# Transposing an even query tile one slot later, together with its odd neighbour

## The chip, the cores and the metric

One core of one Trainium2 chip runs the whole program. The metric is device time in microseconds (us) from start to end of one execution. The engines are named as the profile names them: PE is TensorE's matrix multiply, PEld its weight load, DVE is VectorE, ACT ScalarE, POOL GpSimd, SP the engine that issues the transfers (its queue is SPq).

## The reference, cut to what matters

The input is 32 images of 128 channels by 56 x 56 pixels, float32. Two residual layers follow each other. The first multiplies each channel of the group-normalised image by a gate, which comes from a small deformable convolution over the pooled channels. The second is local attention:

```python
value = conv1x1(x, v_w, v_b)
keyf = proj(x, k...); query = proj(x, q...)       # two 1x1 convs with batch norm and relu each, 64 channels
uk = concat([unfold3(keyf, d) for d in (1, 2, 4)]) # 27 neighbours of each pixel, dilations 1, 2, 4
uv = concat([unfold3(value, d) for d in (1, 2, 4)])
sim = softmax(sum(uk * query[:, :, None], axis=1, keepdims=True), axis=2)
context = sum(sim * uv, axis=2)
return conv1x1(context, w_w, w_b)                  # added to x
```

## The kernel before, in words

**Tiles.** An image is cut into 7 strips of 8 columns, a strip into 7 units of 8 x 8 pixels. Two units are the 128 queries of one tile (128 partitions); 49 units give 25 tiles, 0 to 24, the last one half full. The neighbours of a unit lie in a window of 16 x 16 pixels, so the scores of a tile are 128 queries by 256 keys.

**The path of one tile.** `scores` (L401, one matmul at L416, 256 columns) writes the scores to PSUM (`ps_s`, two banks). `masked` on DVE (L924, L929) adds a mask, takes the row's minimum of the negated scores (`zmin`) and writes `e` in SBUF, a ring of 5 buffers. `exponentials` on ACT (L580, L584) takes the exponential with its row sum. `reciprocals` and `scaled` on DVE (L934, L939; lines 937, 943 and 946) normalise it. `transposed` on PE (L420, L428) turns the 128 x 256 tile into two 128 x 128 transposes, written into a PSUM bank `ps_t` that an even tile and the odd tile after it share. `copy` on ACT (L587, L599) moves both of them, 512 columns, to `eT` in SBUF at once. `context` on PE (L433; L449 and L454) multiplies `eT` with the values into `ps_o`, and `final` on DVE (L950, L954) adds the result to the image.

**The order of the work is written out by hand.** There are 25 slots per image, one per tile, and each engine runs its own list of calls per slot. The stages lag: in slot t, `scores(t)`, `masked(t)` and `exponentials(t)` run; scaling is of tile t - 1, transposing of tile t - 3, context of tile t - 5 (`SCALE, TRANSPOSE, CONTEXT, FINAL = 1, 3, 5, 6`, L45). A lag past the start of an image goes to the last tiles of the image before. On PE the slot is, in this order (L543 to L565): `scores`, `transposed`, then if due `hidden` and `values`, `context`, if due `query_and_key`, and small matmuls of the gate's chain of steps (L505 to L523).

**What prepares the next strips.** Seven times per image PE runs `hidden` (L460, the matmul at L466, 448 columns) for a strip, ACT writes `hid` (L634), in the next slot PE runs `query_and_key` (L469, L471), and ACT writes the keys `kk` (L621) and the queries `qq` (L610), all through one PSUM bank `ps_p`. With `G_SLOT` (L47), `hidden` runs in slots 1, 4, 8, 11, 15, 19 and 22, and `query_and_key` in slots 2, 5, 9, 12, 16, 20 and 23. `values` (L474, L489) runs in slots 4, 7, 10, 17, 18, 21 and 24. One slot later than `query_and_key`, SP copies keys within SBUF: L355 (`kk<-kk`) and, for three tiles whose two units lie in different strips (tiles 3, 10 and 17), L359 and L361 (`ksp<-kk`). `scores` of such a tile waits for them (L404). SP also stores the finished image (`store`, L343, L345) in slot 5 of the next image, ahead of the key copies of slot 6.

**ACT's slot** (L623 to L638): `copy`, if the tile t - 3 is odd or is tile 24, then `exponentials(t)`, then `hid`, or `kk` and `qq`, where due, then steps of the gate's chain (L645, L650). Since tile t - 3 is odd in even slots, the copies come in the even slots 4 to 24, in slot 1 (tiles 22 and 23) and in slot 2 (tile 24 alone).

**DVE's slot** (L1031 to L1050): reciprocal of tile t - 1, `masked(t)`, `scaled` of tile t - 1, chain steps, `final`, and the write-back of the values (L967).

Of the kernel before, what the change touches and what calls it, by code (L numbers as in the profile page):

```python
# [36 lines left out]
TILES = 25  # L37
# [107 lines left out]
def lagged(n, t, lag):  # L145

    return (n, t - lag) if t >= lag else (n + -1, t - lag + TILES)
# [11 lines left out]
def build(nc, x, par, w1, w2, wv, wo, bo, bv, wg, out):  # L159
    with ExitStack() as ctx:  # L160
# [141 lines left out]
        def items_at(n, t):  # L302

            for m, rel in ((n, t), (n + 1, t - TILES)):
                if m.exists():
                    yield m, rel

        def chain_at(n, t):

            for m, rel in ((n + 1, t + TILES), (n + 2, t), (n + 3, t - TILES)):  # L310
                if m.exists():
                    yield m, rel
# [10 lines left out]
        def images(first, last, drain=0, register=None):  # L323

            with nc.Block() as block:
# [74 lines left out]
                def _(pe):  # L400
                    def scores(n, t):  # L401
                        s, u = half_tile(2 * t)
                        if special(t):
                            pe.wait_ge(k_copied[0].sem, k_copied[0].count(n, copies(s + 2)))  # L404
                            pe.wait_ge(q_done.sem, q_done.count(n, s + 2))
                            window = ksp[:, s // 2, :, :]
                        else:
                            if u < 2:
                                g = min(s + 1, STRIPS - 1)
                                pe.wait_ge(k_copied[g % 2].sem, k_copied[g % 2].count(n, copies(g)))  # L410
                                pe.wait_ge(k_copied[(g - 1) % 2].sem, k_copied[(g - 1) % 2].count(n, copies(g - 1)))
                                pe.wait_ge(q_done.sem, q_done.count(n, s + 1))
                            window = kk[:, s:s + 2, UPIX * u:UPIX * (u + 2)]
                        i = (TILES * n.parity() + t) % 2
                        pe.wait_ge(z_done.sem, z_done.count(n, t - 1))
                        nc.tensor.matmul(ps_s[i][:, 0:KEYS].rearrange("p (s h k) -> p h s k", s=2, h=2), qq[:, t, :],  # L416
                                         window.rearrange("p h (s k) -> p h s k", s=2),
                                         start=True, stop=True).then_inc(s_done.next(), 1)

                    def transposed(n, t):  # L420
                        j = t // 2
                        o = ps_t[(EPAIRS * n.parity() + j) % 2]
                        pe.wait_ge(n_done.sem, n_done.count(n, t + 1))
                        if t % 2 == 0:
                            pe.wait_ge(eT_done.sem, eT_done.count(n, j - 1))
                        base = KEYS * (t % 2)
                        for i in range(2):
                            last = nc.tensor.transpose(  # L428
                                o[:, base:base + KEYS].rearrange("p (a s k) -> p s a k", a=2, s=2)[:, i],
                                e[:, t % RING, P * i:P * (i + 1)], ident[:])  # L430
                        last.then_inc(t_done.next(), 1)
# [28 lines left out]
                    def hidden(m, g):  # L460
                        if g == 0:
                            pe.wait_ge(dg.sem, dg.count(m, 17))
                            pe.wait_ge(pg.sem, pg.count(m, 36))
                        pe.wait_ge(q_done.sem, q_done.count(m, g))
                        pe.wait_ge(k_done.sem, k_done.count(m, g))
                        nc.tensor.matmul(ps_p[:, 0:SPIX].rearrange("p (r c) -> p r c", c=SIDE), w1x[:, m.parity(), :],  # L466
                                         strip_of(m, g), start=True, stop=True).then_inc(h_ps.next(), 1)

                    def query_and_key(m, g):  # L469
                        pe.wait_ge(h_done.sem, h_done.count(m, g + 1))  # L470
                        nc.tensor.matmul(ps_p[:, 0:SPIX], w2T[:], hid[:], start=True,  # L471
                                         stop=True).then_inc(qk_ps.next(), 1)

                    def values(m, b):  # L474
                        i = b // 2
                        pe.wait_ge(v_done.sem, v_done.count(m, b))
                        pe.wait_ge(xb_done.sem, xb_done.count(m, min(2 * i + 2, COLUMNS)))

                        held = [k for k, at in CHAIN_READS if CH[at] <= V_SLOT[b]]
                        if held and (m + 2).exists():  # L480
                            pe.wait_ge(dg.sem, dg.count(m + 2, max(held)))
                        if (m + 1).exists():
                            held = [k for k, at in CHAIN_READS if CH[at] <= V_SLOT[b] + TILES]
                            pe.wait_ge(dg.sem, dg.count(m + 1, max(held, default=0)))
                        held = [k for k, at in CHAIN_READS if CH[at] <= V_SLOT[b] + 2 * TILES]
                        pe.wait_ge(dg.sem, dg.count(m, max(held)))
                        for j in range(4 if b % 2 == 0 else CHUNKS - 4):
                            pixels = xb[:, i, 4 * (b % 2) + j, :, :].rearrange("p h k -> p (h k)")
                            last = nc.tensor.matmul(ps_v[:, P * j:P * (j + 1)], pixels,  # L489
                                                    wvox[:, m.parity(), :], start=True, stop=True)  # L490
                        last.then_inc(v_ps.next(), 1)
# [34 lines left out]
                    def tables(t):  # L526
                        if t == CH["c2"] + 1:
                            pe.wait_ge(g_const, N_ID)
                            pe.wait_ge(v_w, 3)
                            nc.tensor.transpose(ps_p[:, 0:P], w1_s[:], ident[:])  # L530
                            nc.tensor.transpose(ps_p[:, P:2 * P], w2_s[:], ident[:])
                            nc.tensor.transpose(ps_p[:, 2 * P:3 * P], wo_s[:], ident[:]).then_inc(t_w, 1)
                        if t == CH["c3"] - 1:
                            pe.wait_ge(v_tab, 3)
                            pe.wait_ge(dg.sem, dg.count(Image(0), 4))
                            nc.tensor.matmul(ps_v[:, 0:P], wv_s[0:HD, :], woT[0:HD, :], start=True, stop=True)
                            nc.tensor.matmul(ps_v[:, P:2 * P], bv_row[0:HD, :], woT[0:HD, :], start=True,
                                             stop=True).then_inc(t_vo, 1)
                        if t == CH["c3"]:
                            pe.wait_ge(v_w, 12)  # L540
                            pe.wait_ge(v_tab, 5)

                    def slot(n, t):  # L543
                        if n.offset == first + 1:
                            tables(t)
                        if n.exists():
                            scores(n, t)
                        m, k = lagged(n, t, TRANSPOSE)
                        if m.exists():
                            transposed(m, k)  # L550
                        for m, rel in items_at(n, t):
                            for g, at in enumerate(G_SLOT):
                                if rel == at:
                                    hidden(m, g)
                            if rel in V_SLOT:
                                values(m, V_SLOT.index(rel))
                        m, k = lagged(n, t, CONTEXT)
                        if m.exists():
                            context(m, k)
                        for m, rel in items_at(n, t):  # L560
                            for g, at in enumerate(G_SLOT):
                                if rel == at + 1:
                                    query_and_key(m, g)
                        for m, at in chain_at(n, t):
                            chain(m, at)  # L565

                    for n, t in slots(first, last, drain, register):
                        slot(n, t)
# [522 lines left out]
```

## Time and profile before

| | |
|---|---|
| median of 3 runs | 1548.74 us (1544.45 to 1551.37) |
| the profiled execution | 1545.68 us, its span 1543.9 us |
| PE busy | 1481.4 us, 96% of the span |
| DVE, ACT, POOL busy | 78%, 76%, 50% |
| share of the chain that ended last | PE 78%, ACT 7%, DVE 5%, issue 5%, DMA 3% |
| mean granted TensorE clock | 0.997 |

The chain that ended last is followed back from the last instruction: at each step to what released it, or to the instruction before it on its engine. A float32 matmul appears as two instructions, a transpose as one. Matmuls are pipelined, so the time from the start of one to the start of the next says more than the duration given for one.

### The profile page before, as it was taken

The page shows a single profiled execution, that of the slowest core. Times are in us where ns is not written, and L with a number is a line of the kernel's source. Part 1 is how long each engine was busy: PE and PEld are TensorE (multiplying, and loading weights), DVE is VectorE, ACT ScalarE, POOL GpSimd, SP SyncE. Part 2 cuts the span into 40 slices and gives each one's busy share as a digit, 9 for nine tenths or more (in the row PEclk, how much of TensorE's full clock was granted, in tenths as well). Part 3 has the DMA queues.
Part 4 walks back from the last instruction along what each step waited for, and adds up shares of the span by engine and source line. Part 5 has one row for each costly group of instructions (what it writes and reads, how often), then busy time and mean ns, then how long its engine had stood idle before and what let it go on. Part 6 is the DMA issues. An engine that isn't in the chain of part 4 may idle for free.

```text
span 1543.9 us, 35552 instructions
## 1 busy us (share of the span) xinstructions
PE 1481.4 (96%) x9287; PEld 1199.6 (78%) x9287; DVE 1211.6 (78%) x4620; ACT 1168.4 (76%) x3044; POOL 776.1 (50%) x2194
## 2 busy tenths in 40 slices
PE   1899999999999999999999999999999999999998
PEld 1587878888887888878888888888887887878776
DVE  6587878888887887878888888888878887878766
ACT  2577777777777777777777777777777777777776
POOL 5544455555465454455454455545455544455520
PEclk9999999999999999999999999999999999999999
DMA  3135453435453445553445553435454445453324
GB/s 132 47 106 160 151 160 114 136 112 162 149 163 107 137 114 154 156 157 113 136 116 155 156 162 113 139 107 162 149 163 119 135 114 154 148 163 113 96 67 138
DMA packets 104276, 205.98 MB, mean 133 GB/s; under 512 B 13584, under 2 KB 83600, under 8 KB 95888
## 3 DMA queue, kind: packets, MB, share of 16 engines
q1 hardware_dynamic: 104080, 203.72, 44.3%
q8 instruction: 80, 1.31, 0.4%
q14 instruction: 116, 0.95, 0.2%
HBM read 51.62 MB, written 51.38 MB: 67 GB/s over the span
## 4 chain that ended last, share of the span: by engine, by line
PE 78%; ACT 7%; DVE 5%; issue 5%; DMA 3%; SPq 1%; POOL 1%; ACTq 0%; DVEq 0%; POOLq 0%
PE ps_s L416 18%; PE ps_o L449 15%; PE ps_p L471 11%; PE ps_v L489 10%; PE ps_p L466 9%; PE ps_t L428 9%; DMA ksp<-kk 3%; PE ps_o L454 3%; ACT eT L599 2%; ACT e L584 2%; DVE e L946 1%; ACT qq L610 1%; ACT hid L634 1%; DVE e L929 1%; SPq L359 1%
## 5 line engine op out<-in xcount | busy, mean ns | idle before, releaser
L584 ACT ACTIVATE e<-e,zmin 128x256 f32<-128x256 f32 x800 | 404.1, 505 | 209.8 <-DVE zmin L929 201.8
L929 DVE CUSTOM_DVE_ANT_0 e<-ps_s,mask 128x256 f32<-128x256 f32 x800 | 337.3, 422 | 150.2 <-PE ps_s L416 144.1
L449 PEld LDWEIGHTS ps_o<-eT,v 128*128 128x128 f32 x2688 | 377.8, 191 | 74.0 <-issue 69.6
L449 PE MATMUL ps_o<-eT,v 128*128 128x128 f32 x2688 | 433.8, 276 | 0.5 <-ACT eT L599 0.3
L416 PE MATMUL ps_s<-kk,qq 128*128 128x256 f32 x1408 | 428.0, 386 | 0.0
L428 PE MATMUL ps_t<-ident,e 128*128 128x128 f32 x1600 | 306.0, 273 | 0.2 <-DVE e L946 0.2
L428 PEld LDWEIGHTS ps_t<-ident,e 128*128 128x128 f32 x1600 | 225.4, 141 | 81.1 <-DVE e L946 0.5
L599 ACT ACTIVATE eT<-ps_t 128x512 f32<-128x512 f32 (+1 forms) x416 | 235.0, 565 | 63.8 <-PE ps_t L428 61.6
L946 DVE SCALAR_TENSOR_TENSOR e<-e,rz,keep 128x256 f32<-128x256 f32 x480 | 251.6, 524 | 0.0
L416 PEld LDWEIGHTS ps_s<-kk,qq 128*128 128x128 f32 x1408 | 221.4, 192 | 35.7 <-issue 29.5
L471 PE MATMUL ps_p<-hid,w2T 128*128 128x448 f32 x448 | 214.6, 561 | 9.7 <-ACT hid L634 9.7
L489 PE MATMUL ps_v<-wvox,xb 128*128 128x128 f32 x1600 | 216.3, 276 | 0.8 <-DVE v L967 0.8
L937 DVE RECIPROCAL rz<-zs 128x1 f32<-128x1 f32 x800 | 126.4, 158 | 112.6 <-ACT e L584 109.2
L489 PEld LDWEIGHTS ps_v<-wvox,xb 128*128 128x128 f32 x1600 | 200.2, 193 | 15.0 <-issue 13.9
L733 POOL TENSOR_TENSOR g<-g,mhalf 128x1 f32<-128x1 f32 x64 | 36.4, 569 | 344.3 <-DVE g L995 244.7
L466 PE MATMUL ps_p<-raw,w1x 128*128 128x448 f32 x448 | 207.5, 545 | 0.9 <-ACT qq L610 0.8
L610 ACT ACTIVATE qq<-ps_p,bn_t 64x256 f32<-64x256 f32 (+1 forms) x448 | 198.1, 442 | 8.4
L800 POOL TENSOR_SCALAR raw<-raw,g 128x448 f32<-128x448 f32 x224 | 167.5, 749 | 37.3 <-PE ps_p L466 37.3
L621 ACT ACTIVATE kk<-ps_p,bn_t 64x448 f32<-64x448 f32 x224 | 141.4, 631 | 39.6 <-PE ps_p L471 26.3
L584 ACT ACTIVATION_READ_ACCUMULATOR e<-e,zmin 128x1 f32 x800 | 150.6, 188 | 0.0
L634 ACT ACTIVATE hid<-ps_p,b1x 128x448 f32<-128x448 f32 x224 | 138.6, 619 | 15.0 <-PE ps_p L466 14.9
L751 POOL TENSOR_SCALAR hats<-hats 128x128 f32<-128x128 f32 x96 | 28.7, 299 | 227.9 <-ACT hats L645 222.3
(147 smaller groups left out, 1917.8 us busy)
## 6 DMA issues: line engine op xcount, KB each, us to landing
raw<-in_x_dram SPq DMA_DIRECT2D x32, 1568.0 KB, 7.2
out_dram<-raw SPq DMA_DIRECT2D x32, 1568.0 KB, 5.4
v<-v SPq DMA_DIRECT2D x192, 224.0 KB, 3.2
kk<-kk SPq DMA_DIRECT2D x192, 112.0 KB, 2.2
ksp<-kk SPq DMA_DIRECT2D x192, 64.0 KB, 2.5
v<-v_last SPq DMA_DIRECT2D x64, 128.0 KB, 2.9
kk<-kk SPq DMA_DIRECT2D x32, 224.0 KB, 2.9
v<-v_last SPq DMA_DIRECT2D x64, 96.0 KB, 2.7
```

What stands on the lines that cost most here:

```text
L416: nc.tensor.matmul(ps_s[i][:, 0:KEYS].rearrange("p (s h k) -> p h s k", s=2, h=2), qq[:, t, :], window.rearrange("p h (s k) -> p h s k", s=2),
L428: last = nc.tensor.transpose(o[:, base:base + KEYS].rearrange("p (a s k) -> p s a k", a=2, s=2)[:, i], e[:, t % RING, P * i:P * (i + 1)], ...
L449: last = nc.tensor.matmul(o[:, UPIX * (u - 1):UPIX * (u + 1)], v[:, s, u, :], eT[:, UPIX * (base + 2 * u - 1):UPIX * (base + 2 * u + 1)], ...
L466: nc.tensor.matmul(ps_p[:, 0:SPIX].rearrange("p (r c) -> p r c", c=SIDE), w1x[:, m.parity(), :], strip_of(m, g), start=True, stop=True).th ...
L471: nc.tensor.matmul(ps_p[:, 0:SPIX], w2T[:], hid[:], start=True, stop=True).then_inc(qk_ps.next(), 1)
L489: last = nc.tensor.matmul(ps_v[:, P * j:P * (j + 1)], pixels, wvox[:, m.parity(), :], start=True, stop=True)
L584: nc.scalar.activation(e[:, i, :], e[:, i, :], ACT.Exp, bias=zmin[:, i:i + 1], scale=-1.0, accum_out=zs[:, i:i + 1]).then_inc(e_done.next( ...
L599: nc.scalar.activation(eT[:, base:base + size], ps_t[(EPAIRS * n.parity() + j) % 2][:, 0:size], ACT.Copy).then_inc(eT_done.next(), 1)
L610: last = nc.scalar.activation(qq[HD * b:HD * (b + 1), at:at + len(units), UPIX * b:UPIX * (b + 1)], src[:, units[0]:UNITS:2, :], ACT.Relu, ...
L800: gp.tensor_scalar(to, to, col(X_A + m.offset % RAWS), col(X_B + m.parity()), ALU.mult, ALU.add).then_inc(x1_done.next(), 1)
L929: nc.vector.tensor_tensor_reduce(e[:, i, :], ps_s[(TILES * n.parity() + t) % 2][:, 0:KEYS], mask[:].rearrange("p s h a b -> p (s h a b)"), ...
L946: nc.vector.scalar_tensor_tensor(e[:, i, :], e[:, i, :], rz[:, i:i + 1], keep[:, KINDS.index(outside(t)), :], ALU.mult, ALU.mult).then_inc ...
```

## The change

On PE, the transposes of an even tile no longer run in their own slot but one slot later, directly ahead of those of the odd tile. Tile 24, the last and even, has no odd neighbour and stays in its slot. In slots 0, 3, 5, 7, 9, ... and 23 PE then has no transposes, in slots 1, 4, 6, 8, ... and 24 it has four, in slot 2 two as before. Nothing changes on the other engines: `copy` on ACT runs in the same slots and waits for the same count.

```diff
                         m, k = lagged(n, t, TRANSPOSE)
-                        if m.exists():
+                        if m.exists() and (k % 2 == 1 or k == TILES - 1):
+                            if k % 2 == 1:
+                                transposed(m, k - 1)
                             transposed(m, k)
```

## Rows read from the trace of the kernel before

**Rows 1.** The page, busy time of each engine, share of the span, instructions.
```profile
PE 1481.4 (96%) x9287; PEld 1199.6 (78%) x9287; DVE 1211.6 (78%) x4620; ACT 1168.4 (76%) x3044; POOL 776.1 (50%) x2194
```
**Rows 2.** The page, costliest groups: count, busy us, mean ns, idle before and releaser.
```profile
L428 PE MATMUL ps_t<-ident,e 128*128 128x128 f32 x1600 | 306.0, 273 | 0.2 <-DVE e L946 0.2
L428 PEld LDWEIGHTS ps_t<-ident,e 128*128 128x128 f32 x1600 | 225.4, 141 | 81.1 <-DVE e L946 0.5
```
**Rows 3.** Waits: engine, output, line, releaser: us in total, times, longest.
```profile
ACT eT L599 <- PE ps_t L428: 61.6, 104, 1.2
...
PEld ps_s L416 <- DMA ksp<-kk: 27.8, 36, 2.6
...
PE ps_p L471 <- ACT hid L634: 9.7, 35, 2.0
PE ps_s L416 <- DMA ksp<-kk: 9.7, 8, 1.9
```
**Rows 4.** Timeline, PE, slots 23 to 2: start us, us, instructions, [idle <-releaser].
```profile
797.23 0.61 PE L449 MATMUL ps_o<-eT,v 128*128 128x128 f32 x4
797.68 0.92 PE L471 MATMUL ps_p<-hid,w2T 128*128 128x448 f32 x2
798.43 0.59 PE L416 MATMUL ps_s<-kk,qq 128*128 128x256 f32 x2
798.87 0.38 PE L428 MATMUL ps_t<-ident,e 128*128 128x128 f32 x2
799.08 0.83 PE L489 MATMUL ps_v<-wvox,xb 128*128 128x128 f32 x6
799.75 0.61 PE L449 MATMUL ps_o<-eT,v 128*128 128x128 f32 x4
...
803.91 0.61 PE L449 MATMUL ps_o<-eT,v 128*128 128x128 f32 x4
804.73 1.02 PE L471 MATMUL ps_p<-hid,w2T 128*128 128x448 f32 x2 [0.20 <-ACT hid L634]
```
**Rows 5.** Timeline, ACT, the same slots.
```profile
796.87 0.61 ACT L634 ACTIVATE hid<-ps_p,b1x 128x448 f32<-128x448 f32 x1
...
798.63 0.63 ACT L621 ACTIVATE kk<-ps_p,bn_t 64x448 f32<-64x448 f32 x1 [0.35 <-PE ps_p L471]
...
800.21 0.60 ACT L599 ACTIVATE eT<-ps_t 128x512 f32<-128x512 f32 x1
...
804.06 0.61 ACT L634 ACTIVATE hid<-ps_p,b1x 128x448 f32<-128x448 f32 x1
```
**Rows 6.** Timeline, PE, slot 9's queries and keys, slot 10's scores; ACT, the `hid` before.
```profile
816.91 0.61 ACT L634 ACTIVATE hid<-ps_p,b1x 128x448 f32<-128x448 f32 x1
...
817.67 0.93 PE L471 MATMUL ps_p<-hid,w2T 128*128 128x448 f32 x2
...
818.43 0.63 PE L416 MATMUL ps_s<-ksp,qq 128*128 128x256 f32 x2
```
**Rows 7.** Timeline, PEld, the weight load of slot 10's scores in two successive images.
```profile
772.23 0.34 PEld L416 LDWEIGHTS ps_s<-ksp,qq 128*128 128x128 f32 x2 [0.41 <-DMA ksp<-kk]
...
818.36 0.30 PEld L416 LDWEIGHTS ps_s<-ksp,qq 128*128 128x128 f32 x2 [0.49 <-DMA ksp<-kk]
```
**Rows 8.** Timeline, SP's queue in slots 5 to 7: the store, then the key copies.
```profile
811.89 0.35 SPq L345 DMA_DIRECT2D out_dram<-raw  x1
812.49 0.46 SPq L355 DMA_DIRECT2D kk<-kk  x1
...
814.43 1.37 SPq L361 DMA_DIRECT2D ksp<-kk  x1
```
**Rows 9.** The transfer issued at 814.43 alone: us from issue to landing.
```profile
DMA to landing us min/median/max: 3.9/3.9/3.9
```
**Rows 10.** Stretches: busy us (instructions) by engine, granted clock, DMA share, GB/s.
```profile
814.00:815.00 1.00, 1.00 (x10) 0.97 (x10) 0.48 (x2) 0.49 (x3) 0.74 (x4) 1.00 0.97 401
...
60.00:80.00 20.00, 19.89 (x106) 14.99 (x105) 13.73 (x51) 13.55 (x36) 13.23 (x41) 0.84 0.24 58
```

## The prediction

> **What bounds the kernel now.** I read four views, in this order. First the busy times [rows 1]: PE is busy for 96% of the span, no other engine for more than 78%. So a change of order pays only where it takes idle time from PE or makes PE's own work shorter. Second the groups of the transposes [rows 2]: 1600 matmuls, two per tile in 800 tiles, and 0.2 us of idle time before all of them together. No transpose waits for its tile today, so putting one off removes no wait of its own. Third the waits [rows 3]: PE's outputs that come late are few. L471 waits for ACT's `hid` 35 times, 9.7 us in total, and the scores of a strip-crossing tile wait for the key copy 8 times, 9.7 us. ACT's `copy` waits for transposes 104 times of 416, 61.6 us, which costs nothing while PE is the bound. Fourth the timeline of one image in mid-run. The image repeats every 46 us: the same weight load stands at 772.23 and at 818.36 [rows 7]. What happens at one place of an image therefore counts some 32 times, and 0.24 us per image is 0.5% of the time. That is about what a measurement of this kernel can tell from no change.
>
> **The length of the work that moves.** In slot 24 the two transposes start at 798.87 and the next work at 799.08 [rows 4]: 0.21 us for two. So twelve times per image 0.21 us of PE time goes from an odd slot into the even one after it (from slot 0 into slot 1 once). The number of transposes, weight loads, waits and signals is the same. No transfer and no instruction of another engine is moved.
>
> **What comes earlier, what comes later.** PE starts its list in an odd slot where it did before. What stands behind the removed transposes there, and the scores of the even slot that follows, are wanted 0.21 us earlier. After the four transposes PE is back on its old time. So the end of the second pair, which `copy` waits for, does not move, and I cost ACT's copy and the exponentials behind it at nothing. The free places are hidden too: a ring buffer of `e` is held one slot longer, but DVE's `masked` of slot t needs scores t first, and PE issues these behind the transposes that free the buffer. The `ps_t` bank of a pair is asked for later than before. The context of an even tile is wanted 0.21 us nearer to its copy; but at least a context and the next scores lie between, 0.4 us each (797.23 to 797.68 and 798.43 to 798.87 [rows 4]), and no wait of context for `eT` stands among those of [rows 3], which are PE's longest behind the start.
>
> The time can then change in three ways.
>
> **(a) Work wanted earlier that cannot come earlier: a loss.** If PE is held at such a place, moved work that could have filled the time is now behind it. The loss is the 0.21 us, less the slack that was there. One place has nearly none: the scores of slot 10, tile 10. Its weight load waits for the copies into `ksp` in every image, also where the matmul is not late: it starts at 818.36, the matmul at 818.43 [rows 6, 7]. PEld's column in the waits says 36 times, 27.8 us [rows 3]. The matmul follows its load within 0.07 us, so the scores have hardly any slack. I take 0 to 0.04 us, 0.02 in the mean. Can the copy land earlier as well? It is issued at 814.43 and lands 3.9 us later, at 818.33 [rows 8, 9]. Ahead of it the finished image is stored from 811.89 on, and the transfer engines' share is 97% in the microsecond from 814 to 815 [rows 10]. The key copy at 812.49 [rows 8] could start perhaps 0.1 us sooner, because `query_and_key` of slot 5 comes sooner. But the store is tied to DVE work which hangs on slot 3 and 4, and that doesn't move. While the store's backlog is drained, an earlier issue does not help, so I take no shift, and keep 0.1 us for the range. The Trainium skill ("DMA: Bandwidth & Descriptors", Queues, rings and completion order) says that on each DMA engine the descriptors of a queue are consumed in ring order; by that rule the shift would be 0, and the trace's 3.9 us for a small copy behind a store agrees. Loss: 0.21 - 0.02 = 0.19 us, times 32 = **+6.1 us**. In the eight images where the copy is late anyway the whole 0.21 is lost, 8 x 0.02 = +0.2 us more.
>
> Other such places have more slack. `query_and_key` starts at the earliest 0.67 us after the start of its `hid` (804.06 and 804.73, a case where it waited [rows 4, 5]). In slot 9 that is 816.91 + 0.67 = 817.58 against 817.67 [rows 6]: 0.09 us of slack. What is lost there is not paid twice, since the scores of slot 10 stop PE behind it anyway.
>
> **(b) A chain that starts earlier: a gain.** In slot 2 PE waits for `hid`. After context it would start at 803.91 + 0.45 = 804.36 (0.45 being 797.23 to 797.68) and it starts at 804.73: 0.37 us lost per image [rows 4]. This `hid` ends a chain on ACT that starts with `query_and_key` in slot 23: `kk` at 798.63 waits for it (0.35 us idle), then `qq`, the copy at 800.21, two exponentials with DVE's mask between, the copy and exponential of slot 1, `hid` at 804.06 [rows 5]. No transpose is late for it: they end at 799.1, the copy is at 800.21. Slot 23 is odd, so `query_and_key` is wanted 0.21 us sooner. It is itself held by `hid` of slot 22: 796.87 + 0.67 = 797.54 [rows 5], against 797.68 [rows 4]. So the chain starts **0.14 us** sooner, and PE, with 0.37 us to give, follows. 31 x 0.14 = **-4.3 us**.
>
> **(c) Fewer changes of kind.** Twelve times per image one entry into the transposes and one exit become a plain handoff. From 798.43 to 798.87 is 0.44 us for 512 columns of scores, which is 0.427 at the rate of 107 ns per 128 (0.21 for two transposes): at most about 0.01 us per handoff. Bounds: 0 and 12 x 0.01 = 0.12 us per image. Most lie in stretches that end in a wait (slots 3 to 9 before the key copy, 13 to 16 and 20 to 2 before `hid`), where nothing is kept. Three remain, slots 11, 17 and 19: 32 x 0.03 = **-1.0 us**.
>
> **Sum.** 6.1 + 0.2 - 4.3 - 1.0 = +1.0 us on the profiled 1545.7, so 1546.7. The profiled execution is 3.1 us below the median of the runs (1548.7); beside the median the forecast is **1549.7 us**.
>
> **Rivals.**
> *Gain kept.* The key copy follows by 0.1 us and all handoffs count, or slot 23 is less held than I read. Then per image 0.09 - 0.14 - 0.12 = -0.17 us, -5.4 us: 1543.3. With no loss at slot 10 it is -0.26, -8.3 us: 1540.4, the only way past -0.5%. For it: PE's wait of 0.37 us is real and larger than what I take from it. Against: the load at 818.36 right behind a landing at 818.33 [rows 7 to 9]. Past the bound: chance 0.1.
>
> *Loss alone.* The chain of (b) is held elsewhere, for instance at DVE, and slot 10 loses in full: 32 x 0.21 = +6.7 us, 1555.4. Against: `kk` at 798.63 stands behind idle time that ends with L471 [rows 5].
>
> *Slower: four transposes run at the pace of their weight loads.* A transpose's load takes 141 ns [rows 2], its streaming 107. A pair can hide the difference behind its neighbours, four in a row may not. Price: twelve groups, in each the two added ones 0.034 us longer: 0.82 us per image, 26 us: 1575. It decides as soon as a load cannot run beside the one before it. Against: six matmuls of `values` in a row, with loads as long or longer, take 799.08 to 799.75, 0.112 each [rows 4]. Chance 0.05.
>
> *The clock.* The granted clock is 0.84 from 60 to 80 us [rows 10], right after the start, and 0.997 in the mean. If longer runs of transposes made it fall again, each per cent of clock would cost about 15 us, since PE is busy for 1481 us [rows 1]; a mean of 0.97 would give 1589 us. No row of this trace shows a fall tied to transposes: they stand in each slot today at full clock. "TensorE: Matmul & The Clock Gate" of the Trainium skill (Part 4: PE-mode transpose) says that transposes don't count as activity of the engine in the way matmuls do; by that rule four in a row speak against the change. They would last 0.43 us here, with matmuls on both sides. Chance 0.02.
>
> **How the numbers follow.** My own case with *loss alone* and the smaller part of *gain kept* lies within 0.5%: 0.79. Faster by more: 0.10. Slower by more: 0.11, from weight loads (0.05), clock (0.02) and *loss alone* with one more odd slot held, each worth up to 6.7 us (0.04). The range reaches from the better end (-7 us) to the worse (+8 us) around the median of before and takes in the spread of the runs: 1542 to 1557.
>
> **What would show it.** In the profile after: four transposes with about 0.43 us from their start to the next work (right for the pace; 0.5 or more means weight loads). `query_and_key` of slot 2 still waits, about 0.2 to 0.25 us instead of 0.37. The scores of slot 10 wait for DMA in nearly all images, some 30 times instead of 8, about 0.2 us more each. ACT's `copy` keeps its idle time of about 62 us. The image period stays within 0.1 us. I am wrong if the wait for `ksp` doesn't grow, if the wait of slot 2 stays the same, or if a new wait shows in an odd slot: PE for `eT` ahead of context, or for `hid` in slot 5.

## The result, and the profile after

| | before | after |
|---|---|---|
| median of 20 runs each | 1550.32 us (1542.77 to 1553.31) | 1556.99 us (1549.45 to 1562.68) |
| the profiled execution, its span | 1545.68, 1543.9 us | 1560.72, 1558.9 us |

The ratio is 1.0053, 95% interval 1.0041 to 1.0066. The medians differ by 6.7 us; the ratio, 1.0053, stands for 8.2 us. I had forecast 1549.7 us, 1.0 us more than before, which can't be told from no change. The median falls on the range's upper edge (1557), but the kernel is slower by more than the measurement is uncertain.

The page after, busy time and the transposes. The fences of this section are of the changed kernel, whose lines behind L549 are two further down.
```profile
PE 1499.5 (96%) x9287; PEld 1223.3 (78%) x9287; DVE 1219.8 (78%) x4620; ACT 1168.3 (75%) x3044; POOL 773.6 (50%) x2194
...
L428 PE MATMUL ps_t<-ident,e 128*128 128x128 f32 x1600 | 244.6, 274 | 0.0
```
PE is busy 18 us longer with the same 9287 instructions (against [rows 1]): its work took longer, it did not only wait. That the transposes' own time fell from 306.0 us [rows 2] is no saving: four in a row overlap, each still takes 274 ns. The waits:
```profile
ACT eT L601 <- PE ps_t L428: 74.6, 104, 2.2
...
PEld ps_s L416 <- DMA ksp<-kk: 30.7, 31, 2.7
...
PE ps_s L416 <- DMA ksp<-kk: 12.0, 9, 2.0
PEld ps_p L471 <- ACT hid L636: 11.9, 36, 2.4
...
PE ps_p L471 <- ACT hid L636: 3.8, 5, 2.0
```
Against [rows 3] PE's late starts for the key copy grew from 9.7 to 12.0 us, the wait of queries and keys for `hid` shrank from 9.7 to 3.8 us, and ACT's `copy` waits 74.6 us instead of 61.6, in as many cases. PE's waits are counted from the modelled end of the matmul before, so that starts which are late by 0.1 or 0.2 us hardly show among them: the timeline has to be read for these.

**An undisturbed image.** Timeline, PE, slots 9 and 10, then 22 to 24, then 2:
```profile
780.86 1.02 PE L471 MATMUL ps_p<-hid,w2T 128*128 128x448 f32 x2
781.73 0.70 PE L416 MATMUL ps_s<-ksp,qq 128*128 128x256 f32 x2
782.26 0.60 PE L428 MATMUL ps_t<-ident,e 128*128 128x128 f32 x4
782.70 1.06 PE L489 MATMUL ps_v<-wvox,xb 128*128 128x128 f32 x8
...
806.66 0.61 PE L449 MATMUL ps_o<-eT,v 128*128 128x128 f32 x4
807.19 1.02 PE L471 MATMUL ps_p<-hid,w2T 128*128 128x448 f32 x2
808.04 0.59 PE L416 MATMUL ps_s<-kk,qq 128*128 128x256 f32 x2
808.48 0.60 PE L428 MATMUL ps_t<-ident,e 128*128 128x128 f32 x4
...
813.74 0.61 PE L449 MATMUL ps_o<-eT,v 128*128 128x128 f32 x4
814.37 1.02 PE L471 MATMUL ps_p<-hid,w2T 128*128 128x448 f32 x2
```
and ACT, the same slots 22 to 2:
```profile
806.52 0.62 ACT L636 ACTIVATE hid<-ps_p,b1x 128x448 f32<-128x448 f32 x1
...
808.25 0.63 ACT L623 ACTIVATE kk<-ps_p,bn_t 64x448 f32<-64x448 f32 x1 [0.31 <-PE ps_p L471]
...
813.70 0.61 ACT L636 ACTIVATE hid<-ps_p,b1x 128x448 f32<-128x448 f32 x1
```
Four transposes take 0.44 us (782.26 to 782.70), so they keep the pace. But look at a matmul that had to wait for its input. `query_and_key` of slot 23 is held by `hid` (806.52 + 0.67 = 807.19) for 0.08 us. The next matmul then starts 0.85 us later, where it was 0.75 us [rows 4, 797.68 to 798.43]. The scores of slot 10 waited for the key copy, and the transposes follow after 0.53 us instead of 0.43. A float32 matmul is two loads and two matmuls, and one that had to wait pays 0.10 us more behind the wait: of `query_and_key` the second matmul starts 0.48 us behind the first, where it is 0.38 us in the cases without a wait.

To compare whole images I took from the timeline every start on PE, less 0.107 us per 128 columns of what ran before it. Of the 30 periods between successive L517 the 20 shortest have a median of 45.98 us before and 46.15 after: **+0.17 us**. In it: slot 9 waits 0.04 us, slot 10 starts 0.10 us later and takes 0.10 more, slots 23 and 24 lose 0.10 and 0.10, slot 2 waits 0.20 instead of 0.38, and all changes of kind together give 0.09. The key copy itself holds the scores of slot 10 back by only some 0.01 us more; what they pay is slot 9's 0.10 and their own.

**The disturbed images.** In both profiles some images are 1.4 to 3.7 us longer, nearly every second one for a stretch. Timeline, PE, one of them after the change, and two windows of it (busy us by engine, granted clock, DMA share, GB/s):
```profile
214.86 1.02 PE L471 MATMUL ps_p<-hid,w2T 128*128 128x448 f32 x2
217.63 0.74 PE L416 MATMUL ps_s<-ksp,qq 128*128 128x256 f32 x2 [1.76 <-DMA ksp<-kk]
218.17 1.06 PE L428 MATMUL ps_t<-ident,e 128*128 128x128 f32 x4
219.02 1.92 PE L489 MATMUL ps_v<-wvox,xb 128*128 128x128 f32 x8
```
```profile
218.00:222.00 4.00, 4.00 (x20) 3.89 (x19) 2.26 (x6) 1.08 (x3) 2.03 (x6) 0.57 0.05 14
222.00:226.00 4.00, 4.00 (x25) 3.12 (x24) 2.75 (x11) 2.17 (x6) 0.00 (x0) 1.00 0.71 171
```
The scores of slot 10 start 2.0 us late, and right behind them the granted clock is at its lower level, 1.2 GHz, for 3.4 us: eight matmuls of values take 1.71 us to the next work instead of 0.89. Such a stretch costs about 1.7 us. There are four in mid-run, behind waits of 2.02, 2.09, 2.16 and 2.20 us; the other two long waits, of 2.05 and 2.22 us, have none behind them. Before the change there is none, not even behind a wait of 2.04 us.

Between the two profiled spans lie 15.0 us. Three sizes can be read: 30 x 0.17 = 5.1 us in all images; 3.0 us in six long waits, whose sum grew from 9.8 to 12.8 us; 4 x 1.7 = 6.8 us of lower clock. That makes 14.9, but that it comes out so well is luck. An image with a long wait is counted in the first size and in the second. And 1.7 us arise at the start, where the change hasn't moved anything yet. Timeline, PE, before, then after:
```profile
46.55 0.94 PE L489 MATMUL ps_v<-wvox,xb 128*128 128x128 f32 x6 [0.84 <-DVE v L967]
47.32 0.92 PE L466 MATMUL ps_p<-raw,w1x 128*128 128x448 f32 x2
```
```profile
46.57 1.65 PE L489 MATMUL ps_v<-wvox,xb 128*128 128x128 f32 x6 [0.84 <-DVE v L969]
48.01 1.70 PE L466 MATMUL ps_p<-raw,w1x 128*128 128x448 f32 x2
```
Six matmuls take 0.77 us in the one and 1.44 us in the other: PE still runs at half pace there in the profile after, and by L517 (61.41 and 63.09) it is 1.7 us behind. The first transposes of all come later still.

### The profile page after: what moved, and what is told of

Read it like the earlier page. It is cut to its first block, busy times and chain, and to the rows that moved or that the text cites. A ratio compares the mean times of both kernels' runs of the same rounds, so it can differ in the third digit from the quotient of the medians.

```text
span 1558.9 us, 35552 instructions
## 1 busy us (share of the span) xinstructions
PE 1499.5 (96%) x9287; PEld 1223.3 (78%) x9287; DVE 1219.8 (78%) x4620; ACT 1168.3 (75%) x3044; POOL 773.6 (50%) x2194
## 3 DMA queue, kind: packets, MB, share of 16 engines
q8 instruction: 80, 1.31, 0.3%
## 4 chain that ended last, share of the span: by engine, by line
PE 82%; DVE 5%; issue 4%; DMA 3%; ACT 3%; SPq 1%; POOL 1%; ACTq 0%; DVEq 0%; POOLq 0%
PE ps_s L416 20%; PE ps_o L449 17%; PE ps_p L471 11%; PE ps_v L489 10%; PE ps_t L428 10%; PE ps_p L466 9%; DMA ksp<-kk 3%; PE ps_o L454 3%; DVE e L931 1%; ACT e L586 1%; DVE e L948 1%; SPq L359 1%; ACT qq L612 1%; PE ps_v L505 1%; PE ps_v L523 1%
## 5 line engine op out<-in xcount | busy, mean ns | idle before, releaser
L449 PEld LDWEIGHTS ps_o<-eT,v 128*128 128x128 f32 x2688 | 391.5, 192 | 89.2 <-issue 64.0
L601 ACT ACTIVATE eT<-ps_t 128x512 f32<-128x512 f32 (+1 forms) x416 | 235.5, 566 | 76.9 <-PE ps_t L428 74.6
L428 PE MATMUL ps_t<-ident,e 128*128 128x128 f32 x1600 | 244.6, 274 | 0.0
L428 PEld LDWEIGHTS ps_t<-ident,e 128*128 128x128 f32 x1600 | 202.2, 141 | 42.3 <-issue 0.6
L489 PEld LDWEIGHTS ps_v<-wvox,xb 128*128 128x128 f32 x1600 | 209.6, 196 | 21.8 <-issue 13.9
L471 PE MATMUL ps_p<-hid,w2T 128*128 128x448 f32 x448 | 220.3, 574 | 4.3 <-ACT hid L636 3.8
L489 PE MATMUL ps_v<-wvox,xb 128*128 128x128 f32 x1600 | 220.2, 279 | 0.8 <-DVE v L969 0.8
```

The costliest lines, as they stand in the source:

```text
L428: last = nc.tensor.transpose(o[:, base:base + KEYS].rearrange("p (a s k) -> p s a k", a=2, s=2)[:, i], e[:, t % RING, P * i:P * (i + 1)], ...
L449: last = nc.tensor.matmul(o[:, UPIX * (u - 1):UPIX * (u + 1)], v[:, s, u, :], eT[:, UPIX * (base + 2 * u - 1):UPIX * (base + 2 * u + 1)], ...
L601: nc.scalar.activation(eT[:, base:base + size], ps_t[(EPAIRS * n.parity() + j) % 2][:, 0:size], ACT.Copy).then_inc(eT_done.next(), 1)
```

## The experiments

Each ran beside the kernel before on the same chip, and ratios are to it. The changes of the order on PE have one form, in which `put_off` lists the tiles:

```diff
-                        if m.exists():
+                        if m.exists() and k not in put_off:
+                            if k - 1 in put_off:
+                                transposed(m, k - 1)
                             transposed(m, k)
```

**Where is the loss made? (only6, not6, not20)** `put_off` is (6,), all even tiles but 6 and 24, and all but 20 and 24.

> Only tile 6 is put off into slot 10; the other tiles stay in their own slots. Theory A (place: the loss is made where the scores of slot 10 wait for the key copy, and the clock drops stand behind long waits there): the image period grows by about 0.20 us in undisturbed images, the granted clock falls to half for 3.4 us behind some of the long waits as in the changed kernel, and the time is 5 to 10 us above before, ratio 1.004 to 1.006. Theory B (grouping: four transposes in a row cost something at each of the twelve places): one twelfth of the loss, under 1 us, ratio 1.000 to 1.001, and hardly any drop of the clock.

> All even tiles but tile 6 are put off. Theory A: the scores of slot 10 wait no more than before, no drop of the clock in mid-run, and the time is that of before within 2 us, ratio 0.999 to 1.001. Theory B: eleven twelfths of the loss stay, ratio about 1.005.

> All even tiles but tile 20 are put off. Theory A, with the reading that the chain from slot 23 to slot 2 gained nothing because the queries and keys of slot 23 waited and then took 0.1 us longer: PE gets 0.2 us back in slots 23 and 24 and waits 0.37 us instead of 0.20 in slot 2, so the time is that of the changed kernel within 1 us, ratio to before 1.004 to 1.006. The prediction on record (the chain gains 0.14 us per image): without that gain the time would be 4 us above the changed kernel, ratio about 1.008.

Measured: only6 1549.95 us, ratio 1.0007 (0.9996 to 1.0018); not6 1556.30, 1.0057 (1.0042 to 1.0073); not20 1562.06, 1.0090 (1.0069 to 1.0110). By their times only6 and not6 came out as theory B says and not as A. Only not20 speaks against B, for it shouldn't be slower than the changed kernel; what refutes B is after_store7 below, where all the groups of four stand and cost nothing that can be measured. The profiles show what hides A. The waits for the key copy, first only6, then not6:
```profile
PE ps_s L416 <- DMA ksp<-kk: 7.7, 9, 1.7
```
```profile
PE ps_s L416 <- DMA ksp<-kk: 18.3, 14, 1.8
```
The undisturbed image is as theory A has it: 46.24 us in only6 (+0.26), 45.99 in not6 (+0.01). But the number of long waits (above 1.2 us) is 3 in only6, 6 before and after the change, 11 in not6 and 7 in not20, with sums of 5.5, 9.8, 12.8, 19.1 and 14.1 us. What one gained in all images it lost in a few, or the other way. So not6, with no loss in the undisturbed image and no lower clock, is as slow as the changed kernel. The lower clock shows three times in not20 and in neither of the others. One thing stays open: not20's profiled execution is as long as that of the changed kernel, 1558.9 us, but its median lies 5 us higher, and nothing in its profile explains that.

**What makes a wait long? (before_pad64, after_pad64)** In the transfer records one packet stands out, 16 KB on the queue of instructions. Transfer queues of the kernel before in two windows (packets, MB, share of the engines): 1277.5 to 1278.8 us, ahead of a long wait, then 1185.5 to 1186.8, the same place of an image without one:
```profile
q1 hardware_dynamic: 293, 0.26, 89.3%
q8 instruction: 1, 0.02, 4.6%
```
```profile
q1 hardware_dynamic: 311, 0.29, 102.9%
```
That queue carries 80 packets in the run, 1.31 MB. PE's program has about 20,650 instructions, so that is one packet for 256 of them or so; with the 64 instructions more of the experiment below it is 81. Eight profiles have the store as before and unhindered: before and after, the three above, the two with padding and after_tail10 below. Of their 256 images 49 have a long wait. In all 49 such a packet starts 0.5 to 1.1 us before the scores of slot 10 are due, in none of the other 207. In the kernel before it takes 0.9 to 1.1 us; which of the 16 transfer engines carries it, the trace doesn't tell. The key copy itself is late there. The landing of the copy issued at 1274.84, ahead of the long wait at 1280:
```profile
DMA to landing us min/median/max: 5.4/5.4/5.4
```
That is 5.4 us instead of 3.9 [rows 9]. Does it depend on where PE's program is cut?

```diff
+                    pe.wait_ge(g_const, N_ID)
+                    for _ in range(32):
+                        nc.tensor.transpose(ps_t[0][:, 0:P], ident[:], ident[:])
```

> The kernel before with 32 unused transposes of the identity, 64 instructions, at the head of PE's program, where PE idles. Theory C (fetch: the long waits for the key copy, 1.3 to 2.2 us, arise where one 16 KB packet of PE's own instructions, 256 of them, runs on a transfer engine 0.5 to 1.1 us before the scores of slot 10 are due; it hits every second image for a stretch because an image has about 640 PE instructions, 2.5 packets): the packets come some 4.6 us of the image earlier, waits above 1.3 us for the key copy become rare (0 to 2 of 32 instead of 6), and the time falls by 5 to 9 us, ratio 0.994 to 0.997. Rival (the long waits have to do with the image's parity, its buffer or HBM alone): 5 to 7 long waits as before, ratio 1.000.

> The changed kernel with the same 64 instructions at the head of PE's program. Theory C: the long waits and with them the half-clock stretches of 3.4 us go, what is left above before_pad64 is the 0.16 us per undisturbed image, 5 us: ratio to before 0.998 to 1.001. Rival: as the changed kernel, ratio 1.004 to 1.007, with half-clock stretches in mid-run.

Measured: 1547.18 us, ratio 0.9993 (0.9978 to 1.0007), and 1561.97 us, 1.0086 (1.0066 to 1.0106). I had expected the long waits to go, and they didn't: 5 and 6 of them. But they moved to other images. Before, they were at 123, 216, 494, 1280, 1374 and 1468 us; with the padding at 630, 725, 818, 1004 and 1098. So it isn't an image's parity or buffer alone, and the packet does follow PE's program; 64 instructions shift which images are hit and do not take the hits away. What decides their number, 3 to 11, I have not settled. In after_pad64 the undisturbed image was 46.22 us and the lower clock came three times. With the padding the change costs 14.8 us between the medians, without it 6.7: where the packets fall moves the price of the change by more than the price of the undisturbed images.

**Take the collision away (before_store7, after_store7).** The store is issued in slot 7, behind the key copies.

```diff
-                        m, k = lagged(n, t, FINAL)
+                        m, k = lagged(n, t, FINAL + 2 if n.exists() else FINAL)
                         if k == TILES - 1 and m.exists():
                             store(m)
```

> The kernel before, with the store of a finished image issued in slot 7 instead of 5 (for the last image still in slot 5), behind the key copies of slot 6. If the store's backlog is what holds the key copy back, the copy lands some 2 to 4 us earlier, the scores of slot 10 never wait for it, and the 9 to 12 us of that wait go: 1539 to 1544 against about 1550, ratio 0.993 to 0.997. If the copy is late for its own sake, the wait stays and the ratio is 1.000.

> The changed kernel with the store of a finished image in slot 7 instead of 5. Where the key copy is never late, the change can cost only what it does elsewhere. By the account of the image in the profile (slots 23 and 24 lose 0.20 us, slot 2 gains 0.18, fewer changes of kind give a little) it is within 1.5 us of before_store7, 1535 to 1538, ratio to before 0.991 to 0.993, and no half-clock stretch stands in mid-run. If the grouping costs something in itself, it stays 5 us or more above before_store7: 1541 or more, ratio 0.995 or more.

Measured: 1536.67 us, ratio 0.9921 (0.9907 to 0.9935), and 1537.16 us, 0.9931 (0.9912 to 0.9950). SP's queue in before_store7, and the landing of the copy of 804.79 alone:
```profile
804.12 0.62 SPq L359 DMA_DIRECT2D ksp<-kk  x1
804.79 0.62 SPq L361 DMA_DIRECT2D ksp<-kk  x1
805.45 0.59 SPq L345 DMA_DIRECT2D out_dram<-raw  x1
```
```profile
DMA to landing us min/median/max: 2.1/2.1/2.1
```
Its issue takes 0.62 us instead of 1.37 and it lands after 2.1 us instead of 3.9 [rows 8, 9], at 806.9, and the scores of slot 10 want it at 809.56. No wait above 1.2 us is left for it and no lower clock in mid-run, with or without the change. And there the change costs nothing that can be measured in the time: 45.99 and 46.05 us per image, 1536.7 and 1537.2 us. The gain, 12 us over the kernel before and 20 over the changed one, is a little more than the 9 to 12 us expected. The store in slot 7 takes away the backlog and, with 2.7 us of slack, also what a packet of instructions could do; it doesn't tell the two apart.

**Why does the chain gain nothing? (store7_only20)** The store in slot 7, `put_off` is (20,).

> The kernel before with the store in slot 7 and only tile 20 put off, from slot 23 into slot 24. The prediction on record: the chain to slot 2 starts 0.14 us sooner and PE follows, 4.3 us faster than before_store7 (1536.7), ratio to before 0.989 to 0.990. What the profile of the changed kernel suggests: queries and keys of slot 23 wait and then take 0.1 us longer, PE loses 0.2 us in slots 23 and 24 and waits 0.2 us less in slot 2: no change within 1 us, ratio 0.991 to 0.993.

Measured: 1537.47 us, ratio 0.9913 (0.9892 to 0.9934): no gain over before_store7. Its timeline, PE, `query_and_key` of slots 23 and 2:
```profile
789.14 1.02 PE L471 MATMUL ps_p<-hid,w2T 128*128 128x448 f32 x2
...
796.34 1.02 PE L471 MATMUL ps_p<-hid,w2T 128*128 128x448 f32 x2
```
From one to the other it is 7.20 us, where before it is 797.68 to 804.73, 7.05 us [rows 4] (7.07 in before_store7). The chain starts sooner and is longer by the same amount, 0.10 us of it in `query_and_key` itself.

**Are other places free? (store7_not6_20)** The store in slot 7, all even tiles put off but 6, 20 and 24.

> The store in slot 7, and all even tiles put off but 6 and 20, the two whose place makes queries and keys (slots 9 and 23) wait for their input. Theory: no wait is added anywhere, and the fewer changes of kind give at most 0.03 to 0.05 us per image: 0 to 1.5 us faster than before_store7, ratio to before 0.990 to 0.992. If grouping costs something in itself it is slower than before_store7.

Measured: 1539.17 us, ratio 0.9931 (0.9912 to 0.9949), where before_store7 has 0.9921 (0.9907 to 0.9935): the intervals overlap, and the 2.5 us between the medians don't show that it is slower. The undisturbed image is 45.95 us, 0.04 less than the 45.99 of before_store7, as expected. That the profiled span is 3.9 us longer (1535.0 against 1531.1 us) comes from the ends of the run: 2.2 us in the second image, where the clock is at its lower level from 59.3 to 66.1 us, which it isn't in before_store7, and 3.0 us in the last one, with a wait of 2.13 us for the key copy at 1513.26 and a lower clock behind it.

A wait that I had excluded is there nevertheless:
```profile
PEld ps_o L449 <- ACT eT L602: 22.7, 68, 0.9
```
It was 1.6 us in 5 times before; in after_store7 it is 15.9 us in 68 times, and there no context is late by it. Here, in slot 0, context of tile 20 starts 0.23 us late: tile 22's transposes are gone from that slot, so context is wanted 0.21 us sooner, and its copy hangs on the chain from slot 23, which without tile 20 put off doesn't start sooner. It costs nothing. Timeline, PE, `query_and_key` of slot 23, the late context, `query_and_key` of slot 2:
```profile
790.51 0.92 PE L471 MATMUL ps_p<-hid,w2T 128*128 128x448 f32 x2
...
793.03 0.60 PE L416 MATMUL ps_s<-kk,qq 128*128 128x256 f32 x2
793.69 0.71 PE L449 MATMUL ps_o<-eT,v 128*128 128x128 f32 x4
...
797.56 1.02 PE L471 MATMUL ps_p<-hid,w2T 128*128 128x448 f32 x2
```
From slot 23 to slot 2 it is 7.05 us as before: what PE waits in slot 0 it waits less in slot 2, 0.16 us instead of 0.38. The same wait of 0.24 us stands in not20, and in neither the changed kernel nor after_store7, where the two edits go together. In all of them the chain from slot 23 sets when slot 2 goes on, and what PE loses or gains in between is taken from its wait there. So not20 has 46.18 us per undisturbed image, as the changed kernel has.

**What brings the lower clock? (after_tail10, before_late)** In the first the four transposes of slot 10 stand behind values (the same edit, with tiles 6 and 7 moved ahead of `context`); in the second no transpose moves, but the store is held until the keys of slot 5 are there.

```diff
                         sp.wait_ge(o_done.sem, o_done.count(m, STRIPS))
+                        if (m + 1).exists():
+                            sp.wait_ge(k_done.sem, k_done.count(m + 1, 5))
```

> The changed kernel with the four transposes of slot 10 behind the matmuls of values instead of directly behind the scores. The waits for the key copy stay as long, 1.9 to 2.2 us where they are long. Theory T (the half-clock stretches come from a wait followed by work that doesn't count, the transposes): they vanish from mid-run, mean clock 0.997, ratio to before 1.001 to 1.003. Theory L (the length of the wait alone): 2 to 4 stretches of 3.4 us stay, mean clock 0.993 to 0.996, ratio 1.004 to 1.007.

> The kernel before, whose store of a finished image also waits for the keys of slot 5 and so starts some 0.6 us later; no transpose is moved. The key copy lands 0.5 us later in every image and PE waits for it in each: 15 to 20 us slower, ratio 1.010 to 1.013, long waits of 1.9 to 2.6 us. Theory L: half-clock stretches appear behind the longest of them, though only two transposes follow. Theory T: none.

Measured: after_tail10 1558.62 us, 1.0067 (1.0043 to 1.0091), mean clock over its runs 0.9941, though the profiled one has none in mid-run, behind five waits of 2.0 to 2.1 us; before_late 1572.87 us, 1.0145 (1.0122 to 1.0168), more than the 15 to 20 us expected. In before_late nearly every image waits about 0.5 us or more and seven waits are 2.2 to 2.7 us long; the lower clock came behind two of them. An eighth, of 1.6 us, has no packet of PE's instructions ahead of it. Timeline, PE, and the windows around it (columns as above):
```profile
1106.16 0.70 PE L418 MATMUL ps_s<-ksp,qq 128*128 128x256 f32 x2 [2.09 <-DMA ksp<-kk]
1106.70 0.39 PE L430 MATMUL ps_t<-ident,e 128*128 128x128 f32 x2
1106.92 1.88 PE L491 MATMUL ps_v<-wvox,xb 128*128 128x128 f32 x8
```
```profile
1104.00:1106.00 2.00, 0.07 (x1) 0.00 (x0) 0.04 (x1) 1.51 (x3) 2.00 (x8) 1.00 0.81 216
1106.90:1110.30 3.40, 3.40 (x16) 3.12 (x15) 2.12 (x6) 1.09 (x3) 1.50 (x4) 0.51 0.01 2
```
Two transposes follow and the clock falls; with none right behind the wait the mean clock of after_tail10 is as low as that of the changed kernel (0.9948). So it goes with the wait and not with the transposes behind it: in mid-run of the profiles no fall stands behind a wait under 2.0 us, and of the 28 of 2.0 us or more 12 have one behind them and 16 have none. What decides between these is open. That before_late has falls with the transposes in their old places speaks against the transposes as their cause; for after_tail10 only the mean clock does. In "TensorE: Matmul & The Clock Gate", Part 4, the Trainium skill says that they don't count as activity like matmuls; no run here shows that this mattered.

## Why the prediction was wrong, point by point

- **Pace of four transposes, no change of the work:** right. 0.44 us for four.
- **ACT's copy:** it waits 104 times as before, but 74.6 us and not the 62 that I named. No run shows that this cost anything.
- **(a), slot 10:** the place was right. The size was too small, and its make-up wrong: only6, which moves nothing else, has +0.26 us for the 0.19 forecast. Of it 0.10 is what `query_and_key` of slot 9 costs by having waited 0.04 us, and 0.10 is the scores' own. I took a late start to cost its lateness alone, and had written off slot 9's wait as paid by slot 10. That the scores would wait for the copy in some 30 images came nearly true, 26 by the timeline (12 before); but the copy holds them 0.01 us longer and not 0.2, and the waits list counts 9.
- **(a), the late images:** this is the first step that failed. I priced them as "the whole 0.21 is lost, 8 x 0.02 = +0.2 us more", as if late were late. There are six, before and after. Their waits are longer by 0.5 us each, from 1.6 to 2.1 us in the mean (not the same images), and behind four of the six the clock fell. I named the clock as a rival by the transposes, at 0.02, and not by the length of PE's waits, though the waits of up to 2.0 us stood in [rows 3] and a clock below 1 in [rows 10].
- **(b), the chain:** this is the second, "-4.3 us", and of the terms of an undisturbed image it is the one that was off most. The start of `query_and_key` in slot 23 does come sooner by the 0.14 us forecast (2.39 us behind the last transposes of the even slot, 804.80, against 2.52). But having waited for its `hid` it takes 0.10 us longer; `kk` stands 1.06 us behind it and not 0.95, and the gain is gone (store7_only20). Slot 2 waits 0.18 us less only because PE comes 0.20 us later. So the 0.2 to 0.25 us that I had named as a sign came true by luck.
- **(c), changes of kind:** -0.09 us per image, within the bounds of 0 and 0.12, above the 0.03 that I took.
- **The sum** per undisturbed image was +0.03 and is +0.17 us, +5.1 us in the run. The clock adds about 2 stretches per run, read from the mean clock of 0.9948 in the 20 runs against 0.9971 in 47 runs of the kernel before: 0.0023 of 1550, 3.6 us. Together 8.7, beside 8.2 by the ratio and 6.7 by the medians. This is an estimate, and it leaves out number and length of the long waits, which I have from one profile each. They weigh as much as the rest: not6 has neither term and is as slow, by 11 long waits, and with padding the same change costs 14.8 us. So it is shown what the undisturbed images lose and why, and that the rest stands behind the late key copy; how much of the 6.7 us another position of the packets would leave is open.
- **Context against its copy:** free, as I said, though not by my argument, that so much work lies between. In slot 0 it is late by 0.23 us as soon as tile 20 isn't put off as well, and it is free there too, because the wait of slot 2 takes it up.

## What to carry to other kernels

Before work is put off past a wait, look up how near the wait is to its limit: the load of the weights waiting for a transfer in every image said that it had no slack, and the better edit was to take the large store out from in front of the small urgent copy. Work that stays in front of a tight input isn't idle time; it is its cover. Between two waits on the same chain, work can be moved at no price and no gain, as between slot 23 and slot 2 here. And when single edits give times that don't add up, compare undisturbed periods apart from disturbed ones: here a period 0.26 us longer, 8 us in the run, stood beside three long waits fewer, and the time moved by 1 us.

## What I had not expected of the hardware

- A float32 matmul of 448 or 256 columns that has to wait for its input, be it only 0.04 us, delays the work behind it by 0.10 us more.
- In 49 of 49 images with a long wait a 16 KB packet of PE's own instructions, of 0.9 to 1.5 us, ran 0.5 to 1.1 us before the scores were due, at the end of a burst of stores and copies; the 64 KB key copy landed after 5.4 to 6.0 us instead of 3.9 in those that I read. "DMA: Bandwidth & Descriptors" (Queues, rings and completion order) of the Trainium skill says that an engine takes turns between its queues packet by packet, which would allow for the packet's own time; the lateness measured is longer than that. Why is not shown.
- Behind a PE wait of 2.0 us or more the granted clock fell for 3.4 us in 12 of 28 cases, at a price of 1.7 us, nearly as much as the wait itself.
